# Routing half of a mixture-of-experts block during the last attention groups, and placing part of the shared expert between two runs of expert tiles

## The reference, cut to what matters

```python
x = L0_attn_x                                   # 4 x 1024 x 128, float32
mod = (_silu(L0_c) @ L0_wmod).reshape(4, 6, 1, -1)
sa, ca, ga, sb, cb, gb = (mod[:, k] for k in range(6))   # ga, gb: magnitude at least 0.25
h = _layernorm(x) * (1 + ca) + sa
x = x + ga * attention(h)                       # 16 heads of 8, rotary, causal, output times W_o
h = _layernorm(x) * (1 + cb) + sb
probs = softmax(h @ wr.T + rb)                  # 7 routed experts
scores, idx = top_k(probs, 2); scores /= scores.sum(-1)
out = expert(h, shared)                         # silu(h @ g.T) * (h @ u.T), times d; inner width 352
for e in range(7):
    out = out + w[..., e] * expert(h, e)        # w is zero where e is not among the two
x = x + gb * out
```

## Time and profile before

| what | value |
|---|---|
| median of three runs | 798.3 us |
| the profiled execution, its own time | 797.6 us |
| its span, first to last instruction | 795.9 us |
| mean granted TensorE clock | 0.947 |
| busy: PE, DVE, ACT, POOL | 686.8, 573.4, 545.9, 342.0 us |
| the fill of the table (one transfer of 5396 KB, issued in quad 14) | 36.1 us to landing |
| w_raw transfers of 176 KB | 2.7 and 3.4 us to landing |

### The profile page before, as it was taken

One profiled execution on the slowest core, in us unless ns is written; L12 is line 12 of the kernel. 1 busy time (PEld: TensorE's weight loads), 2 busy tenths in 40 slices (PEclk: granted clock), 3 DMA queues, 4 the chain that ended last, 5 costly groups with the idle time before them and its releaser, 6 DMA issues.

```text
span 795.9 us, 18082 instructions
## 1 busy us (share of the span) xinstructions
PE 686.8 (86%) x5304; PEld 395.3 (50%) x5304; DVE 573.4 (72%) x2042; ACT 545.9 (69%) x1013; POOL 342.0 (43%) x551
## 2 busy tenths in 40 slices
PE   2986899999999999999999986678869989999970
PEld 1553123333333333333333434567659889999960
DVE  5797889999999999999999834574773323333543
ACT  2785259889989888989888788544325556666640
POOL 1367613232322322232322123235657887666652
PEclk9999569999999999999999999699999999999995
DMA  9246021111111111111110079202233322223425
GB/s 260 83 156 219 1 74 47 39 30 29 47 47 48 47 28 30 41 46 47 48 37 14 1 136 178 68 23 81 63 92 78 82 76 81 66 68 104 131 87 158
DMA packets 64760, 59.46 MB, mean 75 GB/s; under 512 B 10798, under 2 KB 52398, under 8 KB 64668
## 3 DMA queue, kind: packets, MB, share of 16 engines
q1 hardware_dynamic: 58924, 46.85, 23.3%
q0 software_dynamic: 4480, 9.64, 3.4%
q10 hardware_dynamic: 1264, 1.84, 0.7%
HBM read 33.57 MB, written 24.33 MB: 73 GB/s over the span
## 4 chain that ended last, share of the span: by engine, by line
PE 59%; DVE 18%; ACT 9%; issue 7%; DMA 3%; POOL 1%; SPq 1%; ACTq 1%; DVEq 0%; POOLq 0%
PE ps L1658 13%; PE ps L1602 10%; PE ps L1843 9%; PE ps L1681 7%; PE ps L1854 6%; DVE junk L1238 5%; ACT probs L973 5%; PE ps L1864 3%; PE ps L1758 2%; PE ps L1636 2%; DVE junk L1210 2%; PE ps L1750 2%; DMA routed_results_scratch<-y_s,s_dest 1%; PE ps L1831 1%; DVE rot L1193 1%
## 5 line engine op out<-in xcount | busy, mean ns | idle before, releaser
L973 ACT ACTIVATE probs<-ps 128x1024 f32<-128x1024 f32 (+1 forms) x320 | 285.5, 941 | 34.5 <-PE ps L1681 32.1
L1210 DVE CUSTOM_DVE_ANT_0 junk<-ps,tri 128x512 f32<-128x512 f32 (+3 forms) x512 | 218.5, 487 | 13.9 <-PE ps L1602 11.6
L1602 PE MATMUL ps<-ka,qa 61*128 61x256 bf16 (+3 forms) x788 | 186.7, 325 | 10.0 <-DVE rowmax L1210 3.0
L775 POOL TENSOR_SCALAR_AFFINE_SELECT probs<-probs 128x512 f32<-128x512 f32 x128 | 79.7, 634 | 191.8 <-ACT probs L973 191.8
L1658 PE MATMUL ps<-probs,v 128*32 128x512 f32 (+3 forms) x1536 | 157.7, 498 | 1.3 <-POOL probs L775 1.1
L1681 PE MATMUL ps<-qa,ka 64*128 64x512 bf16 (+3 forms) x768 | 144.6, 331 | 7.7 <-ACT probs L973 5.6
L1602 PEld LDWEIGHTS ps<-ka,qa 61*128 61x128 bf16 x788 | 53.0, 95 | 159.8 <-DVE rowmax L1210 80.4
L844 POOL DMA_INDIRECT routed_results_scratch<-y_s,s_dest x76 | 76.2, 1003 | 41.0 <-issue 35.0
L782 POOL DMA_INDIRECT slot_rows_scratch<-rows,slot x64 | 64.1, 1001 | 56.6 <-DVE slot L1393 30.1
L1243 DVE TENSOR_REDUCE leftmax<-ps 128x1 f32<-128x512 f32 x120 | 78.4, 686 | 8.5 <-PE ps L1602 8.5
L1532 DVE TENSOR_TENSOR hid_s<-sg,ps 128x352 f32<-128x352 f32 x76 | 39.6, 521 | 46.2 <-ACT sg L1087 46.0
(11 more groups left out here) (195 smaller groups left out, 1168.4 us busy)
## 6 DMA issues: line engine op xcount, KB each, us to landing
slot_rows_scratch<-cst SPq DMA_DIRECT2D x1, 5396.0 KB, 36.1
srow<-slot_rows_scratch SPq DMA_DIRECT2D x76, 71.0 KB
k_parts_scratch<-qk_parts SPq DMA_DIRECT2D x12, 320.0 KB, 2.7
ka<-k_parts_scratch SPq DMA_DIRECT2D x32, 120.0 KB
q_parts_scratch<-qk_parts SPq DMA_DIRECT2D x12, 256.0 KB, 2.6
qa<-q_parts_scratch SPq DMA_DIRECT2D x32, 96.0 KB
ka<-k_parts_scratch SPq DMA_DIRECT2D x32, 80.0 KB
xs<-in_x SPq DMA_DIRECT2D x4, 512.0 KB, 9.4
```

The lines of the kernel that those rows point to most:

```text
L775: nc.gpsimd.affine_select(out=p, in_=p, compare_op=ALU.is_ge, fill=0.0, base=0, pattern=[[0, HQ], [1, T]], channel_multiplier=-1).then_inc ...
L973: nc.scalar.activation(probs[(n * NS + s) % 4][:, 2 * h:2 * h + 2, 0:UNTIL[s] - FROM[s]], ps[:, 2 * h:2 * h + 2, FROM[s]:UNTIL[s]], ACT.Ex ...
L1210: last = V.tensor_tensor_reduce(out=junk[:, bank - 5, at:at + w], in0=ps[:, bank, at:at + w], in1=tri[:, CH - w:CH], scale=1.0, scalar=LOW ...
L1602: last = MM(ps[:, bank, at:at + w], qa[m][g0:g0 + KS, c0 + q * T:c0 + (q + 1) * T], ka[m][g0:g0 + KS, d0 + k0:d0 + k0 + w], start=True, st ...
```

## The change

Seven edits, all from the middle of the attention on:

1. The ring of quads 14 and 15 is laid out by hand. The first half's rows are normalised there, by VectorE (chunks 0, 1) and GpSimd (chunks 2, 3), transposed ("rows") and multiplied with the router ("router"); its routing runs on VectorE at the end of quad 15, and "counts" plus everything up to `experts(0)` stands ahead of the last "norm".
2. ScalarE takes the square root for the first half in step 1 of quad 15, and the router's exponential in step 8.
3. The table is filled by 12 smaller transfers, in quads 1 to 12.
4. Expert weights are loaded into `w_whole`, which lies where `w_lo` will be, all 14 transfers in a row; `w_raw` loses its second buffer.
5. Before the tiles only chunks 0 to 3 of the shared expert are done. Chunks 4 to 7 come after the first 38 tiles, then the other 38.
6. The second half's routing is cut into 13 pieces, one in each of the first half's tile steps from 1 on. The first half's 32 scatters are no longer paced by `hidden`; of the second half's, 16 run along with tile steps 22 to 37 and 16 after them.
7. The first half's chunks are transposed for the shared expert after their modulation, so they need one copy instead of two on ScalarE.

```diff
+FIRST_HALF = [(16, "turn", 0), (18, "turn", 1), (20, "project", 0), (22, "turn", 2), (24, "project", 1), (26, "turn", 3),
+              (28, "project", 2)]
+SECOND_HALF = [(0, "project", 3), (2, "turn", 4), (4, "turn", 5), (6, "project", 4), (8, "project", 5), (9, "rows", 0),
+               (11, "rows", 1), (12, "router", 0), (14, "rows", 2), (15, "router", 1), (17, "rows", 3), (18, "router", 2),
+               (20, "router", 3)]
-    units = {NQ - 2: range(4), NQ - 1: range(4, 2 * (B - 1))}.get(n, ())
...
+    late = {NQ - 2: FIRST_HALF, NQ - 1: SECOND_HALF}.get(n, ())
+    plan += [(slot, kind, n, None, u) for slot, kind, u in late]
...
-[("last", [(None, "norm", NQ - 1, None, 1)])]
+[("last", [(None, "counts", NQ - 1, None, 0), (None, "norm", NQ - 1, None, 1)])]
 # SP
+                if 1 <= n <= PADS:
+                    t0, t1 = ST * (n - 1) // PADS, ST * n // PADS
+                    sp.dma_start(slot_d[t0 * T:t1 * T, :] ...).then_inc(s_pad_out, 16)
             sp.wait_ge(s_ring_free, len(BY_DVE))
+            for e in range(NE):
+                sp.dma_start(w_whole[:, e, 0, :], sw_g_d[1 + e, :, :]).then_inc(s_wraw[e], 16)
+                sp.dma_start(w_whole[:, e, 1, :], sw_u_d[1 + e, :, :]).then_inc(s_wraw[e], 16)
+            sp.wait_ge(s_scatter[0], 16 * TOP * GT)
+            for t in range(STG):
+                load_rows(t)
             read_results(0)
+            sp.wait_ge(s_scatter[1], 16 * TOP * GT)
+            for t in range(STG, ST):
+                load_rows(t)
 # POOL
+            def normalise_rows(n):
+                pool.wait_ge(s_rstd2, 1)
+                nc.gpsimd.tensor_tensor(rows[:, ts, 0:D], xs[:, ts, :], mean[:, ts].unsqueeze(2).to_broadcast((T, CG, D)),
+                                        ALU.subtract).then_inc(s_centred, 1)
+                nc.gpsimd.tensor_tensor(rows[:, ts, 0:D], rows[:, ts, 0:D], rstd[:, ts].unsqueeze(2).to_broadcast((T, CG, D)),
+                                        ALU.mult).then_inc(s_xn2_pool, 1)
+                    if n == NQ - 1 and s == CHUNK_END[0]:
+                        for u in range(GC // 2, GC):
+                            normalise_rows(u)
             quads(pool, body)
+            for n in range(GC):
+                modulate_rows(n)
-                pool.wait_ge(s_hid, len(IC) + 1 + x // 2)
...
+                if g == 0 and STG - ALONG <= s < STG:
+                    scatter_second(s - STG + ALONG)
+            slot_steps(0, -2, 3, slot_step)
+            for x in range(ALONG, TOP * GT):
+                scatter_second(x)
 # ACT
+                    if s == 1 and n == NQ - 1:
+                        deviation(0)
+                    if s == 8 and n == NQ - 1:
+                        exp7(0)
...
             modulate2(0)
             modulate2(1)
+            deviation(1)
+            for n in range(GC, NC):
+                normalise(n)
             modulate2(2)
             modulate2(3)
+            first_part(0)
+            silu(0)
...
+            slot_steps(0, -1, 2, slot_step)
+            for n in range(GC, NC):
+                silu(n)
+            slot_steps(1, -1, 2, slot_step)
 # DVE
+                elif kind == "counts":
+                    incl = prefix(0, bank)
+                    end = starts(0, incl)
+                    slots(0, incl, bank)
+                    dve.sem_inc(s_ring_free, 1)
+                    experts(0, end)
+                if done == ("project", NQ - 1, None, GC - 1):
+                    variance(GTILES[0], s_var2)
+                elif done == ("turn", NQ - 1, None, GC + 1):
+                    scale2(0)
+                    for n in range(GC // 2):
+                        normalise(n)
+                elif done == ("router", NQ - 1, None, GC - 1):
+                    softmax_shift(0)
+                elif done == ("norm", NQ - 1, None, 0):
+                    softmax_scale(0)
+                    beaten(0, range(NE))
+                    ranks(0)
+                    weights(0)
+            def route_second():
+                softmax_scale(1); beaten(1, range(4)); beaten(1, range(4, NE)); ranks(1); weights(1)
+                modulate_rows(4); modulate_rows(5); modulate_rows(6); modulate_rows(7)
+                prefix(1, GROUPED); starts(1, incl); slots(1, incl, GROUPED); experts(1, end)
+                if g == 0 and s >= 1:
+                    next(routing, None)
 # PE
             quads(pe, body)
+            ring_write(RING_AT["last"][0])
             values_product(5, 0, NS - 2)
             values_product(5, 0, NS - 1)
+            ring_write(RING_AT["last"][1])
...
+            gate_up(0)
+            turn_rows(4)
+            turn_rows(5)
+            gate_up(1, (0,))
             down(0)
+            router(4)
+            router(5)
+            gate_up(1, (1, 2))
...
+                if g == 0 and s == 7:
+                    pe.wait_ge(s_sel, GRP)
+                    group_counts(1, GROUPED).then_inc(s_prefix, 1)
+            slot_steps(0, -1, 2, slot_step)
+            for n in range(GC, NC):
+                gate_up(n)
+                if n > GC:
+                    down(n - 1)
+            down(NC - 1)
+            slot_steps(1, -1, 2, slot_step)
```

More of the change, by code:

```diff
@@ L426, in adaln_block @@
         s_exp7 = sem("s_exp7")
-        s_wraw = [sem(f"s_wraw{m}") for m in range(2)]
+        s_wraw = [sem(f"s_wraw{e}") for e in range(NE)]
         s_whi = sem("s_whi")
@@ L1435, in _ @@
+            variance(GTILES[1], s_var2)
             scale2(1)
             second2(2)
-            softmax_scale(0)
-            ranks(0)
+            second2(3)
             hidden(0, 0)
-            weights(0)
+            second_part(0)
             hidden(0, 1)
-            incl = prefix(0)
             hidden(0, 2)
-            end = starts(0, incl)
+            second_part(1)
+            second2(4)
+            second2(5)
+            logits(4)
+            logits(5)
+            shared_sum(0)
@@ L1480, in _ @@
[L1480 to L1495 removed]
+            shared_sum(1)
+            hidden(2, 0)
             second_part(4)
[L1497 removed]
@@ L1498, in _ @@
-            hidden(7, 1)
+            hidden(2, 1)
+            hidden(2, 2)
             second_part(5)
-            hidden(7, 2)
-            shared_sum(6)
+            shared_sum(2)
+            hidden(3, 0)
             second_part(6)
-            shared_sum(7)
+            hidden(3, 1)
+            hidden(3, 2)
+            shared_sum(3)
+            def route_second():
+                softmax_scale(1)
+                yield
+                beaten(1, range(4))
+                yield
+                beaten(1, range(4, NE))
+                yield
+                ranks(1)
+                yield
+                weights(1)
+                yield
+                for n in range(GC, NC):
+                    modulate_rows(n)
+                    yield
+                incl = prefix(1, GROUPED)
+                yield
+                end = starts(1, incl)
+                yield
+                slots(1, incl, GROUPED)
+                yield
+                experts(1, end)
+                yield
@@ L1605, in row_scores, with group_counts @@
                 return last
+            def group_counts(g, bank):
+                for name, at in (("before", 0), ("ones", 1)):
+                    c0, w = CST[name]
+                    last = MM(ps[:, bank, at * GT * NE:(at + 1) * GT * NE], cst[:, c0:c0 + w],
+                              sel[:, GTILES[g], :].rearrange("p t e -> p (t e)"), start=True, stop=True)
+                return last
             def ring_write(x):
```

522 lines of the change are left out of this document (215 added, 307 removed).

## The result

The changed kernel takes 810.1 us (median of 4 runs, 807.82 to 811.23) against 798.3 for the kernel before, a ratio of 1.0142 with a 95% interval of 1.0118 to 1.0167. It is slower by 1.4%. The prediction was 807 us; the result lies inside its range and on its side.

What follows compares the result with a forecast made beforehand. TensorE was taken as full in quads 14 and 15, with a chain hopping between engines from attention to tiles. Terms -2.0 + 10.6 + 11.3 - 46.1 + 35.3 = +9.1 gave about 807 us, range 801 to 813.

Steps and rivals of the forecast that it cites:

- Quad 14: Attention's second-last quad: TensorE loses two turns and a projection ahead of the shift; -2.0 us, bounds 0 and -2.5.
- Quad 15: Attention's last quad: added TensorE work, a wait in the ring and blocking between VectorE and GpSimd; +10.6 us, bounds 3 and 12.
- The 2 us for blocking: In quad 15: VectorE and GpSimd normalise at the same moment, four clashing pairs; up to 3.3 us, taken as 2.
- Last exponential to division: Attention's end: VectorE's serial routing +7.3 while TensorE stands, plus 4 for blocking beside GpSimd's modulation; +11.3 us.
- rival B: Quad 15 and attention's end: no blocking between VectorE and GpSimd, 6 us less, kernel 801 us; chance 0.12.
- A: Rival: routing is cheap in quad 15 and up to the division, kernel faster at about 792 us; chance 0.27.
- Division to first tile: Last division to first tile's silu: only four shared chunks remain, 62.5 us against 108.6; -46.1 us, bounds -54 and -38.
- Both covered: Between division and first tile: the weights' 14 transfers and the 32 scatters end early enough not to delay the tiles.
- Rival D: Four-chunk stage before the tiles runs at TensorE's own pace, no waits and full clock; kernel 799 us; chance 0.05.
- Tiles and four chunks: Both tile groups with four shared chunks between: 203.9 us against 169.0 now; +35.3 us, bounds 28 and 43.
- The sign that I named: Between tiles 37 and 38: a silu gap of about 38 us with a wait for the row load at its end.
- rival C: Second half's first tile is late because scatters land 8 us later; 817 us with full blocking; chance 0.13.

Runs made afterwards that it cites:

- e4: Kernel before with only the ring's turn and project pieces at the changed kernel's slots, no routing in the quads; ratio 0.9980 to the kernel before.
- e1: Changed kernel with GpSimd's four modulations of the first half moved inside quad 15; ratio 1.0070 to the kernel before.
- e3: Changed kernel with the second half's 16 early scatters spread two per three steps over steps 15 to 37; ratio 1.0078 to the kernel before.
- e8: Changed kernel with TensorE's new quad 15 pieces (transposes of normalised rows, router products) issued twice; ratio 1.0462 to the kernel before, on a slower chip.
- e5: Changed kernel with modulation inside quad 15, division ahead of the counts and early scatters spread; ratio 1.0345 to the kernel before, on a slower chip.
- e2: Changed kernel with the last division and batch ahead of the first half's counts, prefix, starts, slots and experts; ratio 1.0051 to the kernel before.
- e10: Changed kernel with modulation early, scatters spread and routing pieces cut, division still behind the counts; ratio 1.0246 to the kernel before, on a slower chip.
- e11: Changed kernel with modulation early, scatters spread, routing pieces cut, division ahead of counts, prefix and starts right behind it; ratio 1.0303 to the kernel before, slower chip.
- e12: Changed kernel with modulation early, scatters spread, routing pieces cut, division ahead of counts, prefix and starts behind it, repeated on another slower chip; ratio 1.0264 to the kernel before.
- e9: Changed kernel itself, unedited, run again on a slower chip where the kernel before took 831.0 us; ratio 1.0355 to the kernel before.

## Why the prediction was right, step by step

The direction came from a sum of terms with large opposite signs, and each came out near its size: in the order of the prediction -2.5, +9.4, +14.0, -45.9 and +37.7, with +0.2 at the end, 12.9 in all (predicted -2.0, +10.6, +11.3, -46.1, +35.3, 9.1 in all). Three figures of it don't follow from what stands beside them. Quad 15 takes 21.0 us in the kernel before and not 21.5; 203.9 less 169.0 is 34.9 and not 35.3; and the 1.8 us that TensorE was to wait in the middle would be 2.7 by its 27.8 and GpSimd's 30.5. None moves the sum by more than 1 us.

*Quad 14.* Right: -2.5, and e4 shows that the slots alone move it by 1.95. The rest is within what runs of one list differ by (e1 to e3 begin quad 15 at 460.71 to 462.13).

*Quad 15, predicted +10.6, measured +9.4.* The 8.6 for TensorE's work and the wait in the ring are near the 9.4. TensorE waits 1.05 us for VectorE's copy ahead of router 0 and 1.1 in two places before it, 2.2 for the 1.9 reckoned. That all 6.7 us of work are paid is likely, not shown: e8 rules out slack for all of its added work, but half of what it added at the full clock was absorbed. The 2 us for blocking did not come: VectorE's normalising ran at 0.69 us an instruction (469.06 to 471.81), because GpSimd's stood behind step 2's masks until 473.02. I had taken both to start together. So the price of such a clash in the quad stays open. And the size is in part luck: quad 15 took 30.4, 31.9 or, in e5, 35.0 us in runs of the same list for TensorE, at a granted clock of 1.00, 0.87 and 0.67 from 479 to 492.

*Last exponential to division, predicted +11.3, measured +14.0.* Mechanism right, one term too small. The serial chain was 8.0 (reckoned 7.3), the blocking 6.0 by e1 (taken as 4, with 7 as the bound of eight waits). I had split the difference because one row alone showed it; the row was typical. By the rule of the Trainium skill's page "SBUF — State Buffer", section "Who interferes with whom", it would have been 7, nearer to the 6.0. The trace agrees with a second sentence of that section too, that a copy can take the shared pair: the copies of 128x7 to 128x56 took 0.86 to 1.16 us. That rival B, no blocking, was wrong is shown; A, routing cheap at the attention's end, fell with quad 15 and this stretch together at 23.4 us, where the break-even was 12.8.

*Division to first tile, predicted -46.1, measured -45.9.* Right in size, and the ScalarE chunks are the wait as reckoned. "Both covered" holds for the scatters here; e2, with the slots behind the division, shows the end of that cover, at a price of 3.8 us. Rival D asked for the full clock and no waits; it did not come.

*Tiles and four chunks, predicted +35.3, measured +37.7.* The total was near by luck in part: one wait that was reckoned did not come, and others came that were not. In the first group I put 2 us on routing pieces and 4 on GpSimd's backlog. TensorE's steps show 5.3 us above the pace in the first fourteen, 3.4 of it at prefix, starts and slots, and 1.3 in the last two; e3 takes out just those 1.3. I had summed VectorE's work over all steps, where single pieces of 1.9 to 3.2 us exceed a step's 1.3. In the middle I reckoned 38.5 and it took 43.1: the backlog, which I had put into the steps, held the drain instead (7.0 for 4.7), then the first ten gate products ran at the low clock (4.4 us for 2.3), `shared_sum` held the last down for 0.87, and about 1 more is spread over the chunks' pieces. The 1.8 us of waiting for rows did not come. Of the low clock's 2.1, e1 and e3 show that it can be absent. The sign that I named, a wait for the row load at the middle's end, is not there: the load landed at 695.6 and TensorE was at its last down until 697.0. With that, rival C is wrong in its mechanism, though by 1.4 us only.

## What to carry to other kernels

Before moving serial work ahead of a step that everything waits for, look for an idle window of the same engine behind it: VectorE had 7 us free after the division and did the counts before it, which e2 prices at 7.3 us on its chip (on e10's and e11's it was lost again before the first tile). When VectorE works in short dependent instructions, keep GpSimd's elementwise work out of that stretch: an instruction blocked by it took 0.86 to 1.29 us here, however small, about as long as one of GpSimd's (1.18 to 1.29). And cut work that is slipped between the steps of a loop by the largest piece against the free time of one step, not by the sum against all of them; here that was worth 2.3 us in the steps concerned.

## What the hardware showed that was not expected

Chips differ in more than noise. On three of the four chips of e1 to e12 the kernel before took 830 to 834 us, and on the one of them where the changed kernel ran it took 860.5, against 798 and 810. Between e9 and the changed kernel's first run, quad 15, the stretch to the division and the second group of tiles are alike within 1.5 us (the table); the differences stand where GpSimd issues scatters into `slot_rows_scratch`: 22 us before the first tile, 15 in the first group, 12 in the middle. In e9, first TensorE, then ScalarE:

```profile
526.85 0.39 PE L1776 MATMUL ps<-h_lo,ws_hi 128*128 128x512 f32 x1
554.79 0.74 PE L1776 MATMUL ps<-h_hi,ws_hi 128*96 128x512 f32 x1 [27.55 <-issue]
```

```profile
539.40 1.28 ACT L1017 ACT_TABLE_LOAD   x1
553.42 0.60 ACT L1017 ACTIVATE sgs<-ps 128x512 f32<-128x512 f32 x1 [12.74 <-remote]
```

ScalarE stands 12.7 us behind a table load, until some 3 us after the first half's last scatter was issued at 549.86, and 6.0 us once before (to 538.11). TensorE's 27.6 are its wait for `hidden`, which waits for this silu; on the first chip the same wait took 10.3. GpSimd's own scatters keep 0.96 us each. What I wrote in the expectation of e9, that the scatters themselves land late, is not what the trace shows: the first loads of gathered rows were there at 555 us, as in the changed kernel on the first chip, and in e5, one of the runs that the expectation speaks of, 5 us after the last scatter's issue (557.41 and 562.58). It is the other engines that stand, ScalarE first, for nothing on the core that the profile shows. The cause stays open, and no trace of the kernel before from such a chip was taken, so where its own 32 us lie is not known. A layout that puts scatters beside other work, as the change does, is worth less on such chips: the ratio is 1.0355 there and 1.0142 here.

TensorE's clock fell with TensorE busy. In e8's second half of quad 15 the granted clock was 0.66 in a window where TensorE had work for 23.8 of 25.3 us: it was 0.50 from 479.0 to 489.3, 1.00 to 492.6 and 0.50 again to 498.0, with work all the time. In e5, with the changed kernel's own list for TensorE, it was 0.50 from 477.4 to 484.2, after 7.4 us in which TensorE had work for 5.7 and waited at most 1.05 at a time. Over 479 to 492 that list ran at 1.00, 0.87 or 0.67, and quad 15 was 30.4, 31.9 or 35.0 us long.
